# First attention of a four-stage network: closing and turning transposes set next to the values, and the bank of the sums lent to the scores from step 4

## What is computed

```python
q = _qdq(layernorm(x)) @ _qdq(wq).T + bq
k, v = jnp.split(cond @ wkv.T + bkv, 2, axis=-1)          # 16 heads of 32
attn = jax.nn.softmax(jnp.einsum('bnhd,bmhd->bhnm', q, k) * scale, axis=-1)
o = jnp.einsum('bhnm,bmhd->bnhd', attn, v).reshape(B, N, C)
out = _qdq(o) @ _qdq(wp).T + bp
```

## Time and profile before

| what | value |
|---|---|
| median of 3 runs | 2578.29 us (2577.19 to 2578.38) |
| the profiled execution's own time | 2578.61 us |
| its span in the trace | 2576.8 us |
| TensorE matmul busy | 2514.3 us, 98% |
| VectorE busy | 1790.2 us, 69% |
| GpSimd busy | 1287.2 us, 50% |
| ScalarE busy | 1232.3 us, 48% |

### The profile page before, as it was taken

How to read it: one execution, slowest core, us unless ns; L and a number is a source line. 1 busy time by engine, 2 the same in 40 slices (tenths; PEclk the granted TensorE clock), 3 DMA queues, 4 the chain that set the end, 5 groups by cost and what they waited for, 6 DMA issues and landing times. The chain is left out here.

```text
span 2576.8 us, 33913 instructions
## 1 busy us (share of the span) xinstructions
PE 2514.3 (98%) x13273; PEld 1624.6 (63%) x13288; DVE 1790.2 (69%) x2456; ACT 1232.3 (48%) x1853; POOL 1287.2 (50%) x340
## 2 busy tenths in 40 slices
PE   8999999999999999999999999999999999999998
PEld 8988888987545545545444787888533333335786
DVE  4554544556767767767774676664799999999873
ACT  4222312311666666666664232222588888886110
POOL 0000000001999999999993000000499999997310
PEclk9999999999999999999999999999999999999999
DMA  8677776655545345344313754542997777776400
GB/s 302 212 253 239 266 276 242 217 178 157 114 87 112 72 93 111 68 97 106 68 67 118 259 188 135 175 156 85 253 213 162 167 160 167 156 172 193 125 33 33
DMA packets 218864, 405.10 MB, mean 157 GB/s; under 512 B 18216, under 2 KB 94536, under 8 KB 218640
## 3 DMA queue, kind: packets, MB, share of 16 engines
q1 hardware_dynamic: 218704, 402.93, 56.6%
HBM read 260.63 MB, written 140.59 MB: 156 GB/s over the span
## 5 line engine op out<-in xcount | busy, mean ns | idle before, releaser
L1473 POOL TENSOR_TENSOR pooled<-pooled,probs 128x2048 f32<-128x2048 f32 x140 | 640.7, 4576 | 21.0 <-ACT probs L1334 0.9
L1334 ACT ACTIVATE probs<-psum 128x512 f32<-128x512 f32 (+1 forms) x832 | 458.3, 598 | 334.9 <-PE psum L1226 330.1
L1361 DVE TENSOR_REDUCE win_max<-psum 128x1 f32<-128x802 f32 x480 | 455.1, 988 | 150.5 <-PE psum L1191 150.5
L2258 DVE TENSOR_SCALAR probs<-psum,bound 128x1024 f32<-128x1024 f32 (+1 forms) x416 | 498.8, 1275 | 31.0 <-POOL pooled L2290 21.3
L2233 ACT ACTIVATE probs<-probs 128x1024 f32<-128x1024 f32 (+1 forms) x416 | 437.5, 1059 | 81.9 <-DVE probs L2258 39.6
L2290 POOL TENSOR_TENSOR pooled<-pooled,probs 128x2048 f32<-128x2048 f32 x92 | 424.2, 4611 | 12.8 <-ACT probs L2233 0.4
L1226 PE MATMUL psum<-q_st,k_st 128*128 128x512 f32 (+1 forms) x832 | 333.0, 437 | 18.7 <-ACT probs L1334 12.2
L312 POOL TENSOR_TENSOR r_q<-ve_q,minus_half 128x4 f32<-128x4 f32 x8 | 9.1, 1132 | 611.2 <-DVE ve_q L256 611.2
L1226 PEld LDWEIGHTS psum<-q_st,k_st 128*128 128x128 f32 (+1 forms) x832 | 148.4, 185 | 241.2 <-ACT probs L1334 179.9
L1191 PE MATMUL psum<-k_st,q_st 96*128 96x402 f32 x960 | 265.4, 358 | 6.6 <-DVE o_sb L1380 5.0
L2201 PE MATMUL psum<-q_st,k_st 128*128 128x512 f32 (+1 forms) x832 | 252.7, 430 | 10.1 <-DVE probs L2258 7.8
(11 more groups left out here) (276 smaller groups left out, 4217.1 us busy)
## 6 DMA issues: line engine op xcount, KB each, us to landing
k_st<-k_hi SPq DMA_DIRECT2D x64, 801.0 KB, 10.4
k_st<-k_lo SPq DMA_DIRECT2D x48, 801.0 KB, 10.8
k_hi<-kt_hi SPq DMA_DIRECT2D x32, 801.0 KB
k_lo<-kt_lo SPq DMA_DIRECT2D x32, 801.0 KB
v_rows<-v_out SPq DMA_DIRECT2D x96, 256.0 KB
v_st<-v_rows SPq DMA_DIRECT2D x24, 768.0 KB
q_st<-q_hi SPq DMA_DIRECT2D x64, 256.0 KB, 7.7
w<-w_hi_d SPq DMA_DIRECT2D x64, 256.0 KB, 3.1
```

Of the source, the lines that this page charges most:

```text
L1334: A.activation(probs[i % NPROBS][0:rows, j, :], bank(score_banks.where["score", u, t, j])[0:rows, :], ACT.Exp, scale=1.0 / ROOT).then_inc( ...
L1361: V.tensor_reduce(win_max[:, r, j, c:c + 1], window(windows.where["max", u, i])[:, :, 0:MV], AX.XY, ALU.max).then_inc(max_done, 1)
L1473: G.tensor_tensor(pooled[u % 2][:], before[:], probs[tile(u, k) % NPROBS][:], ALU.add).then_inc(pool_added, 1)
L2258: V.tensor_scalar(probs[i % NPROBS][0:rows, half * W:half * W + W, :], window(("score", u, t, half))[0:rows], bound[0:rows, u // NG, t:t + 1],
```

## The change

Three edits, all in attention_0. three_banks() allows bank 7 for the scores from step 4 on. On TensorE closing() and turn() stand between values() and the third score matmul of their step, and not behind the fourth. On VectorE closing() comes after the first two windows of step 4 and ahead of the third.

```diff
--- before.py
+++ after.py
@@ -1147,7 +1147,7 @@
                     return (u - 1) * HPG * RT * 2 + i
 
                 def three_banks(u, t):
-                    return 5 <= t < pooled_tiles(u) + LAG
+                    return 4 <= t < pooled_tiles(u) + LAG
 
                 def window_of(i):
                     j, rest = divmod(i, RT * 2)
@@ -1303,15 +1303,15 @@
                             if behind[1] == LAST_SUM and behind[0]:
                                 last_sum(behind[0] - 1)
                         if now:
+                            if now[1] == CLOSE_AT and now[0]:
+                                closing(now[0] - 1)
+                            if now[1] == TURN_AT and now[0] + 1 < UNITS:
+                                turn(now[0] + 1)
                             scores(*now, 2)
                         if coming[2:]:
                             max_of(*coming[2])
                         if now:
                             scores(*now, 3)
-                            if now[1] == CLOSE_AT and now[0]:
-                                closing(now[0] - 1)
-                            if now[1] == TURN_AT and now[0] + 1 < UNITS:
-                                turn(now[0] + 1)
                             if now == (UNITS - 2, TURN_AT):
                                 quantising()
                             if now == (UNITS - 1, CODES_AT):
@@ -1437,11 +1437,13 @@
                     V.memset(ones[:], 1.0).then_inc(set_up, 1)
                     V.wait_ge(own.sem, s)
                     for now, behind in steps():
-                        if now and now[0] + 1 < UNITS:
-                            for i in windows_at(now[1]):
-                                max_of(now[0] + 1, i)
+                        coming = [(now[0] + 1, i) for i in windows_at(now[1])] if now and now[0] + 1 < UNITS else []
+                        for one in coming[:2]:
+                            max_of(*one)
                         if now and now[1] == CLOSE_AT and now[0]:
                             closing(now[0] - 1)
+                        for one in coming[2:]:
+                            max_of(*one)
                         if now and now[1] == TURN_AT - 1 and now[0] + 1 < UNITS:
                             turn(now[0] + 1)
                         if now == (UNITS - 2, TURN_AT - 1):
```

## The result

The change makes the kernel slower: 2604.11 us (median of 4 runs, 2603.7 to 2604.85) against 2578.34 us, a ratio of 1.0096 (95% interval 1.0083 to 1.0108). Run once more beside the experiments it stood at 2601.87 against 2579.92, 1.0087 (1.0072 to 1.0102). So it costs 22 to 26 us. The first time is inside the range of 2592 to 2606 and 4.1 above the forecast of 2600.0; the loss of the second comparison, 21.95, is close to the 21.7 of the forecast.

A forecast was written before the change was run, and what follows sets the result against it. TensorE, busy 98% of the span, was taken as the bound, with GpSimd close behind in this stage. Closing with bank wait 14.6, unit 15 0.45 and turn 6.6 made 21.7; 2578.3 + 21.7 = 2600.0 us, range 2592 to 2606.

The forecast's parts named there:

- Bank 7 at t=4: Units 1 to 14: the first score matmul of key tile 4 waits for ScalarE's copy of bank 7, 1.08 us later.
- The lower end of that term: Units 1 to 14: the usual step's 0.41 us wait swallows part of the delay, leaving 0.67 a unit, 9.4 in all.
- Closing next to V(4): Closing beside step 4's value matmuls: VectorE's chain decides, 0.04 of 1.08 us comes back; 14 x 1.04 = 14.6 us.
- Unit 15: Last unit, without maxima: the closing now precedes step 4's third score matmul, so the next values come 0.45 us later.
- Turn next to V(11): Beside step 11's value matmuls, units 0 to 14: four transposes all on the path, 0.44 us each time, 6.6 us.
- The rival that adds up whole transposes: Score matmuls and reciprocal wait for transposes one after another: turns cost 16.3 us, total 2609.7 us; chance 0.04.
- The next steps fall into the usual ring: After step 5's values, steps follow the usual loop through VectorE (3.52 us a step); no further cost was counted.
- The sum: Whole stage: 14.6 + 0.45 + 6.6 = 21.7 us slower, with nothing given back later.
- The marks: Signs of being right: a unit of about 49.3 us, GpSimd idle near 2.3 at its start, stage end about 1419.

The follow-up runs named there:

- e1_bank_only: Only the loan of bank 7 from step 4, on the kernel before; closing and turn in their old places: 2596.94 us, ratio 1.0066.
- e4_early_copy: The whole changed kernel, with ScalarE copying bank 7 between the second and third exponential of step 3: 2586.53 us.
- e2_closing_only: Only the closing moved, on TensorE and VectorE, on the kernel before; bank 7 still from step 5: 2579.88 us, ratio 1.0002.
- e6_late_first: As e4_early_copy, but bank 7 is lent only from the second score matmul of step 4 on: 2587.14 us.

## Why the prediction was right, and where it was off

**Bank 7 at t=4: right.** The forecast was a wait of S0(4) until 0.05 after the copy's end, 1.08 later than before. Measured: 0.05 behind the copy, and 1.09 a unit, 15.3 us. e1_bank_only shows it by itself, e4_early_copy takes it away by making the copy early. The lower end of that term, a usual wait of 0.41 that swallows part of the delay, was not met.

**Closing next to V(4): right.** Walked to +1.04 for both steps together, measured 1.09, since the 0.04 that was to come back did not. As e2_closing_only shows, that step stays at 4.76 because the earlier transposes and the later maximum cancel within the trace's 0.01. The transposes begin, as walked, 1.00 after V(4). Reciprocal and product follow 1.20 and 1.57 us after them; they were walked at 1.14 and 1.51.

**Unit 15: half of it.** The 0.45 of the closing is there (0.44), but 0.48 more came at step 8 to 9.

**Turn next to V(11): right in its mechanism, a little dear.** 0.44 was forecast, 0.39 measured (5.9 us and not 6.6). The rival that adds up whole transposes, 1.09 a turn, is out: they overlap, as the 0.60 for four had said.

**The step that was missing.** "The next steps fall into the usual ring" was wrong at one place: where the loan of bank 7 ends. Thirty-two matmuls rotated over three banks before, thirty-six now. When the scores fall back to banks 0 and 1, it depends on the remainder by three whether the next of these two was taken two or three matmuls ago, and so whether S0 or S1 has to wait. That is 14 x 0.13 = 1.8 us (units 0 to 13), and 0.48 in unit 15, where it is twenty against sixteen. e6_late_first shows it, with thirty-five and nineteen: the same remainders as before, the same step lengths as before.

**The sum.** In the stage: 15.3 for the wait, 0.1 for the closing, 0.9 for unit 15, 5.9 for the turn, 1.8 for the rotation, less 0.07 in unit 0, where bank 7 is free: 23.9, of which the stage's end shows 23.7 (1397.11 to 1420.82) against 21.7 forecast. So the term for the turn was 0.7 too high and the missing rotation 2.3, which partly cancel. Behind the stage the forecast was zero. The span grew by 25.4, so 1.7 more stand there in the profiled execution. About half of it arises at the place shown above, and half near 1864 us, where TensorE's clock fell in all three executions (a granted 0.76 from 1860 to 1867 in this one). The second execution of the same kernel does not have the 1.7, so they are scatter that goes with the clock and no work of the change.

**The marks.** A unit is 49.5 us long (from V(2) at 929.14 to the next unit's at 978.63) against 49.3 forecast, GpSimd idles 2.41 at its start against 2.3, and the stage ends at 1420.8 against 1419.

## What to carry to other kernels

A buffer lent for longer is free only when its last reader has finished, and a pool that hands out the one taken longest ago gives the returning buffer to the very first user. So look where that last reader stands in its own engine's list, and move the reader first. Short work on a full engine was cheapest here where the engine waits for another one anyway, and it was not hidden ahead of what that other one waits for. The turn's four transposes cost 0.39 us more in the new place, while the step that had them in the old one (2.57) was no longer than its neighbour without them (2.61). The closing's eight cost 1.24 us at step 4 and 0.40 us at step 10. And count what rotates modulo the number of buffers at each place where that number changes.

## What the runs showed of the hardware

- Four transposes of 128 x 128 in fp32 take 0.60 us from the first's start to the last's end, though one lasts 0.27; put on the ring of scores and exponentials they lengthen it by 0.39 us.
- Around an idle of 2.00 us TensorE's clock fell in one execution and not in another of the same kernel: sixteen transposes took 3.65 us (a granted 0.50) in one and 1.94 us (1.00) in the other. That makes 1.5 us of scatter at one place of this kernel, and it was not foreseen. What decides it in an execution stays open; no run here varied it on purpose.
